# A new written-out order of turns and banks for four gated layers on one core

## The chip, the cores and the metric

The kernel runs on one core of a Trainium2 chip. The metric is the device time of one execution in microseconds (us). Three runs of the kernel before are shown; their median is the number that a change is held against.

## The reference, cut to what matters

Eight sequences (batches) of 256 rows with 128 features pass through four layers. Each layer adds a gated attention and a gated feed-forward part:

```python
x = x + tanh(g_xattn[0]) * attention0(layernorm(x), ctx)       # 16 heads of 8
x = x + tanh(g_ffn[0])   * depth0(layernorm(x))                # the best 3/4 of the rows pass a block
x = x + tanh(g_xattn[1]) * attention1(layernorm(x), ctx)
x = x + tanh(g_ffn[1])   * moe1(layernorm(x))                  # 8 experts, top 2, and a shared one
x = x + tanh(g_xattn[2]) * attention2(layernorm(x), ctx)       # causal
x = x + tanh(g_ffn[2])   * moe2(layernorm(x))                  # 8 experts of 512, top 2, and a shared one
x = x + tanh(g_xattn[3]) * attention3(layernorm(x), ctx)       # only chosen queries count
x = x + tanh(g_ffn[3])   * quantised3(layernorm(x))            # FP6 blocks
```

The change touches none of this. What matters is that every batch goes through the same long chain of small steps, and that the steps of different batches may be mixed freely.

## The kernel before, in words

**Streams.** Each batch is a stream of some 300 steps (`stream_steps`, L123 on), a list of tuples (step, layer, part): `stats` and `norm` (layer norm), `turn` (transposes), `query` and `keys` (products, then a split of each value into three bf16 parts on POOL, then transfers into `q_st` and `k_st`), `maxima` (scores for the row maxima, 8 tiles a layer), `max_parts`, `max_turn`, then eight `attend` (scores turned, exponential on ACT) and eight `weigh` (weighted sums of the values), `heads`, `heads_turn`, `project`, and the feed-forward steps. Four batches are in flight at a time, in four slots of buffers; batch b + 4 takes the slot of batch b.

**The order.** `TURNS_TAKEN` (L165) is a string of 2,410 digits. Each digit names the batch whose next step comes next. `schedule()` turns it into one list of steps, and each engine's program walks that list and issues its part of each step. So the order on TensorE, DVE, ACT, POOL and on SP's list of transfers is fixed when the kernel is built, and an engine that waits holds up all that stands behind on its own list. `BANKS_TAKEN` (L262) gives, in the same order, which of the eight PSUM banks each use takes, and from it the wait for the reader of that bank before (`bank_holders`). `SCRATCH` (L284) says in front of which steps TensorE runs how many products of zeros (`scratch`, L990 on, the product itself is L997); they write into the bank that the step is about to take, and keep the engine busy while it would wait. All three were worked out ahead of time by a planner that gives each instruction a cost; the planner is no part of the kernel.

**The routed tiles.** The third layer's feed-forward routes the rows of two batches together. When both batches of a pair (0/1, 2/3, 4/5, 6/7) have their router's choice, `place` (nine small DVE steps, L1455 to L1503) works out for each row its place among 15 tiles of 128 rows. `scatter` (L764) is eight indexed transfers from POOL that write the rows into `x_rows`. `fetch` brings them back as tiles, `turn_in` transposes them, and each tile passes `rows_hidden` (L1266, Gelu on ACT L965) and `rows_out` (L1276, copied by DVE L1751), with its expert's weights copied by POOL (`weights`, L776). `keep` writes the results into `y_rows`; `collect` (L783) is four indexed transfers a batch from POOL that gather each row's two results, and `join` adds them on DVE (L1757). POOL issues an indexed transfer itself and does nothing else meanwhile.

**Other work on the lists that the text names.** POOL also does the causal mask of the third layer's attends (the select of L790: `attend` of layer 2), the power for row norms (`key_rows` and `query_rows`, L806), the three operations of each split (L714, L717, L719), and the norm (L724, L731). In layer 3, `choose` picks the queries on DVE in 14 steps (L1623, L1625). ACT changes its function table when Gelu and the exponential alternate (ACT_TABLE_LOAD). `max_clear` and the moves into `q_st` and `k_st` stand on SP's list.

In the texts, "attend 4 of batch 7" is the step ("attend", 7, 2, 4), batch, layer and part.

Of the kernel before, what the change touches and what calls it, by code (L numbers as in the profile page):

```python
# [165 lines left out]
0003020312103121100122002000000001110103101101312132010002100010112103020202220222003100311011312031  # L166
1321231012130103113311303001320123020201021022120203200010121222110221021232111131133212221332030030
3200201312303332232032022202223310110201201100101310103303010320032210001210121120121122211301201001
3011122031222212323023211130202210303030021331013200200202020311231021210211100101211330010033321110
2030121233010232112122122122111223220302100012030022203112102110021000211100032012001001111330201110  # L170
0210211001133003001013331122100113301012123032133220121300001300000213333101131000113101101021132003
0210132130112022020103220121123113121312313133223232311313113323033131211123131111131112111311111111
1311111111111112212111311111113111211101121123323023302323203100230103012303333221123133320013303310
0003333003333313111301303003113333030033013210023033033233132133121010303131303033033300001000330023
3101100010131301101001101131130101131011111011111012033011031003033301033103331131313003010130001303
3311111333331313133301333333331300443413313433343433553335333354425442444544342224242454455325453332
4555454435532425322445242454522445423433524252424545522325353255345232322422422554423223225322442332
5232232243242452225442224443224233435343232323332343335233342225245333232523523233233325522343433222
6453364636543654645354543455435363543536445363445364434635463564466344466434666643637774574564745657
6656446656465656466565774566746565756475474556457764556747654654654775546655666767456666746564444545  # L180
5567546445547754547757576647755476776747765555775754574566655656755765755775464557467566547676664664
5665647446577767646774767746446664576576556465455564644666676546466445657666557465754746666577566675
7564676575565464775454767475657475775744775554475775646764747565466475655565747655455775555545575454
4476647476475666557555755656767567574566556657747775775777665777566555776557776655765555555555555755
5755565555555655577555577775557756555756577665777755557565765777756775677477467776767546777567474765
7477767774564667776576777775475777777777744674657757545567775755574775575757777775777777777577777477
7774444477777777757777777744547777777444777555555544455457446545544454555575464666454574555474457464
4665547544754554455767666666667774776756665646467476774767664766776766566566646765466466757766564767
6675677476576677476774775745766767775747677477656777664745475676766745646567476776674757675767774746
6657476757  # L190
# [87 lines left out]
5064751263704512673013452670123456760123745601237451603245163024516370245163702541637024516370245162  # L278
3701456237045126730451236701450423671540236014523760164502370156423742013567420135674203567423567423
5167425106725167023516723015612756230016723501670341256073412067512034120673420651734206174206145723  # L280
106451230647512306417
"""


# [1580 lines left out]
```

How the kernel before makes its waits and increments, by code:

```python
        @block.sync  # L616
# [13 lines left out]
                sp.dma_start(dst, src).then_inc(values_loaded, 16)  # L630
            for s in range(1, SLOTS):
                load_x(s, s)
                load_ctx(s, s)
            w = Walk()
            for w.i, (step, b, l, part) in enumerate(SCHEDULE):
                s = b % SLOTS
                if step == "load_x" and b + SLOTS < BATCHES:
                    sp.wait_ge(sems["xb_ready"], w.at_step("xb_ready", 1, "max_parts", b, 0, 0))
                    load_x(b + SLOTS, s)
                if step == "load_ctx" and b + SLOTS < BATCHES:
                    sp.wait_ge(sems["a_full"], w.at_step("a_full", 1, "keys", b, LAYERS - 1, 0))
                    load_ctx(b + SLOTS, s)
                if step == "load_weight3" and b == 0:
                    sp.wait_ge(sems["a_full"], w.at_step("a_full", 1, "key_mean", b, SPARSE, 0))
                    sp.dma_start(w3_sb, w3).then_inc(w3_loaded, 16)
                if step in ("keys", "query"):
                    name, terms, st, parts = (("k", K_TERMS, k_st[s], k_parts[s]) if step == "keys"
                                              else ("q", Q_TERMS, q_st[s], q_parts[s]))
                    if b < SLOTS and l == 0:
                        sp.wait_ge(*CLEARED[s])
                    if step == "keys" or b >= SPLIT_STREAMS or l > 0:
                        sp.wait_ge(sems[f"hi_ready{s}"], w.at(f"hi_ready{s}", 1))
                        move_parts(sp, terms, 0, st, parts, sems[f"{name}_moved{s}"])
```

## Time and profile before

| | before |
|---|---|
| median of 3 runs | 939.13 us (937.61 to 941.51) |
| profiled execution | 939.72 us, its span 938.0 us |
| mean granted TensorE clock | 0.961 of full speed |
| busy: TensorE, DVE, POOL, ACT | 827.9, 701.4, 596.0, 587.1 us |
| products of zeros in the written-out order | 207 (and 7 at the start) |

The span runs from the first to the last instruction; what lies around it belongs to the execution's time. Times in rows are us from the span's start, if not marked ns. A granted clock of 1.00 is 2.4 GHz, of 0.5 it is 1.2 GHz; a stretch's number is the mean over it.

### The profile page before, as it was taken

To read this page: it belongs to the slowest core of one execution; us is meant where nothing else is said; L and a number is where in the kernel's file an instruction comes from. 1 tells how busy PE (TensorE), PEld (TensorE's weight loads), DVE (VectorE), ACT (ScalarE), POOL (GpSimd) and SP (SyncE) were. 2 spreads that over 40 slices of the span, in tenths; PEclk is the share of its full clock that TensorE was granted. 3 is DMA by queue.
4 is the path that set the end of the run, shared out by engine and by line. 5 is a ranking of instruction groups with operands and counts; after the bars stand their busy time and mean duration, and the time that the engine had idled before them with its cause. 6 is when DMAs were issued, how large, how long until landed. Compare 5 with 4: busy or idle time off the path is not lost.

```text
span 938.0 us, 21784 instructions
## 1 busy us (share of the span) xinstructions
PE 827.9 (88%) x7627; PEld 525.7 (56%) x7627; DVE 701.4 (75%) x2168; ACT 587.1 (63%) x1454; POOL 596.0 (64%) x751
## 2 busy tenths in 40 slices
PE   8698899989889769997897899989999985797796
PEld 4244358845679425693344357646577954593333
DVE  7997978975752579668999998888683515746997
ACT  2586786567767436762784587776776674268180
POOL 6437548869677785667556537465878658755634
PEclk9898999999999978999999999999999998999698
DMA  5523433221121211223102121111112111311100
GB/s 137 137 77 109 122 105 91 70 64 41 46 67 33 74 35 28 70 64 82 31 21 58 42 54 39 34 36 37 28 45 66 42 49 40 88 36 41 28 4 23
DMA packets 89578, 53.90 MB, mean 57 GB/s; under 512 B 10103, under 2 KB 86416, under 8 KB 89472
## 3 DMA queue, kind: packets, MB, share of 16 engines
q1 hardware_dynamic: 82608, 40.27, 16.2%
q0 software_dynamic: 4272, 10.98, 4.1%
q10 hardware_dynamic: 2592, 1.26, 0.5%
q8 instruction: 63, 1.03, 0.5%
q14 instruction: 43, 0.35, 0.1%
HBM read 17.15 MB, written 9.04 MB: 28 GB/s over the span
## 4 chain that ended last, share of the span: by engine, by line
PE 38%; DVE 24%; POOL 16%; ACT 7%; issue 7%; DMA 5%; SPq 1%; POOLq 0%; DVEq 0%; ACTq 0%
DVE mx L1639 11%; PE banks L1059 5%; PE banks L1266 4%; PE banks L1276 4%; PE banks L1195 4%; POOL h L731 3%; ACT probs L899 3%; PE banks L1023 3%; POOL probs L783 3%; PE banks L1045 3%; PE banks L1010 3%; POOL x_rows L764 2%; PE banks L1003 2%; PE banks L1205 2%; POOL rn L806 2%
## 5 line engine op out<-in xcount | busy, mean ns | idle before, releaser
L1639 DVE TENSOR_REDUCE mx<-banks 128x4 f32<-128x1024 f32 (+1 forms) x240 | 282.9, 1214 | 17.5 <-PE banks L1023 14.1
L899 ACT ACTIVATE probs<-banks 128x512 f32<-128x512 f32 (+1 forms) x512 | 258.3, 587 | 54.8 <-PE banks L1045 53.1
L1059 PE MATMUL banks<-probs,v_aug 128*9 128x256 f32 (+1 forms) x2048 | 151.0, 374 | 16.4 <-ACT probs L899 7.2
L1023 PE MATMUL banks<-k_st,q_st 64*128 64x256 bf16 (+1 forms) x1024 | 93.3, 279 | 32.5 <-DVE mx L1639 14.5
L724 POOL TENSOR_TENSOR rstd<-veps,mhalf 128x2 f32<-128x2 f32 x64 | 46.5, 728 | 105.0 <-DVE veps L1586 104.2
L830 ACT ACTIVATE hT<-banks 128x256 f32<-128x256 f32 (+1 forms) x128 | 47.9, 383 | 102.7 <-PE banks L1003 85.1
L1045 PE MATMUL banks<-q_st,k_st 64*128 64x256 bf16 (+1 forms) x1024 | 93.9, 268 | 6.8 <-DMA q_st<-mT 3.5
L731 POOL TENSOR_SCALAR h<-xs,mv,rstd 128x128 f32<-128x128 f32 x112 | 91.7, 824 | 5.9
L806 POOL TENSOR_TENSOR rn<-ss,mhalf 128x32 f32<-128x32 f32 x16 | 88.0, 5501 | 10.3 <-DVE ss L1373 10.3
L714 POOL TENSOR_TENSOR resid<-resid,parts 128x256 f32<-128x256 f32 x64 | 42.9, 670 | 62.2 <-ACT resid L866 61.8
L1023 PEld LDWEIGHTS banks<-k_st,q_st 64*128 64x128 bf16 x1024 | 36.0, 96 | 82.1 <-DVE mx L1639 23.8
L1195 PE MATMUL banks<-hT,fc_sb 128*128 128x256 f32 x320 | 78.2, 389 | 0.0
L1045 PEld LDWEIGHTS banks<-q_st,k_st 64*128 64x128 bf16 x1024 | 33.5, 94 | 76.0 <-issue 29.5
L1059 PEld LDWEIGHTS banks<-probs,v_aug 128*9 128x9 f32 x2048 | 33.1, 89 | 73.8 <-ACT probs L899 28.4
L756 POOL TENSOR_TENSOR xs<-xs,raw 128x256 f32<-128x256 f32 x72 | 52.5, 730 | 25.8 <-ACT raw L940 23.0
L1276 PE MATMUL banks<-wall,probs 128*128 x480 | 64.2, 277 | 1.0 <-ACT probs L965 1.0
L790 POOL TENSOR_SCALAR_AFFINE_SELECT probs<-probs 128x512 f32<-128x512 f32 x64 | 40.5, 647 | 37.9 <-ACT probs L899 37.8
L1195 PEld LDWEIGHTS banks<-hT,fc_sb 128*128 128x128 f32 x320 | 58.9, 193 | 8.9 <-issue 1.1
L1751 DVE COPY raw<-banks 128x128 f32<-128x128 f32 x60 | 17.0, 288 | 61.6 <-PE banks L1276 61.5
L1276 PEld LDWEIGHTS banks<-wall,probs 128*128 128x128 f32 x480 | 58.5, 192 | 2.9 <-issue 2.7
L861 ACT ACTIVATE parts<-banks,bcol 128x256 bf16<-128x256 f32 x64 | 30.3, 474 | 43.5 <-PE banks L1073 20.9
L997 PE MATMUL banks<-zeros 128*128 128x512 bf16 x214 | 56.1, 409 | 0.0
(232 smaller groups left out, 1774.5 us busy)
## 6 DMA issues: line engine op xcount, KB each, us to landing
k_st<-parts SPq DMA_DIRECT2D x192, 64.0 KB, 2.1
q_st<-parts SPq DMA_DIRECT2D x186, 64.0 KB, 2.1
wall<-in_w POOLq DMA_DIRECT2D x16, 256.0 KB, 3.5
y_rows<-raw SPq DMA_DIRECT2D x28, 128.0 KB, 2.0
raw<-x_rows SPq DMA_DIRECT2D x12, 256.0 KB, 3.6
x_rows<-zeros SPq DMA_DIRECT2D x2, 960.0 KB, 6.6
fc_sb<-in_fc POOLq DMA_DIRECT2D x6, 256.0 KB, 4.1
x_in<-in_x SPq DMA_DIRECT2D x8, 128.0 KB, 3.8
```

Source lines behind the costliest of these rows:

```text
L731: ins = nc.gpsimd.tensor_scalar(h[s][:, r, :], (x_in if l == 0 else xs)[s][:, r, :], mv[s][:, r, 0:1], rstd[s][:, r:r + 1], ALU.subtract, ...
L756: nc.gpsimd.tensor_tensor(xs[s][:, :, :].rearrange("p t d -> p (t d)"), xs[s][:, :, :].rearrange("p t d -> p (t d)"), raw[s][:, n % OUT_RI ...
L806: nc.gpsimd.tensor_tensor(rn[s][:, :], ss[s][:, :], mhalf[:, :], ALU.pow)\
L830: nc.scalar.activation(dst, src, func).then_inc(sems["b_read"], 1)
L899: nc.scalar.activation(probs[s][:, part % UNIT_RING, 2 * a:2 * a + 2, 0:n], b_bank(w, a + 1)[:, 0:2 * n].rearrange("p (j q) -> p j q", j=2 ...
L997: nc.tensor.matmul((a_bank if kind == "a" else b_bank)(w, 1).rearrange("p (h q) -> p h q", h=2), zeros[:, 0:P], zeros_twice, start=True, s ...
L1023: ins = nc.tensor.matmul(a_bank(w, a + 1)[:, i * keys:(i + 1) * keys], head_rows(q_st, s, a, hp0 + i, r * P, P), head_rows(k_st, s, a, hp0 ...
L1045: ins = nc.tensor.matmul(b_bank(w, a + 1)[:, j * n:(j + 1) * n], head_rows(k_st, s, a, 2 * g + j, t * P, P), head_rows(q_st, s, a, 2 * g + ...
L1059: ins = nc.tensor.matmul(c_bank(b, l, u // 4)[VW * i:VW * i + VR, g % 2, q0:ROWS], v_aug[s][:, t, 4 * g + i, :], probs[s][:, u % UNIT_RING ...
L1195: ins = nc.tensor.matmul(a_bank(w, k + 1)[:, a * ROWS:(a + 1) * ROWS], fc1_sb[:, 2 * part + k, a, :], hT[s][:, :], start=True, stop=True)
L1276: ins = nc.tensor.matmul(a_bank(w, 1)[:, 0:D], rows_mid(b, part)[:, c, :], second[:, c * D:(c + 1) * D], start=c == 0, stop=c == HC - 1)
L1639: nc.vector.tensor_reduce(mx[s][:, r, :, hp0:hp0 + n], banks[:, first:first + 2, :].rearrange("p a (n k) -> p a n k", n=n), AX.X, ALU.max) ...
```

## The change

The three constants are written anew; the program around them stays as it is. Core of the diff:

```diff
 TURNS_TAKEN = """
-0003020312103121100122002000000001110103101101312132010002100010112103020202220222003100311011312031
...
+0002011123300231010103020000000001002111102113301100110012100200112210023002031031013310131012022121
...
 BANKS_TAKEN = """
-1023546016724350167234015623016745231067450201673452301672345670134570163745260123456012364503612703
...
+1023545670123457120634125634017562301474567232045132670134506715340156724536017356470134756340123451
...
 SCRATCH = {
-    ("query", 0, 0, 0): 7, ("turn", 1, 0, 0): 19, ("query", 2, 0, 0): 3, ("max_turn", 0, 0, 0): 4,
-    ("attend", 0, 1, 0): 4, ("attend", 1, 2, 0): 2, ("attend", 3, 2, 0): 10, ("maxima", 0, 3, 0): 2,
-    ("attend", 0, 3, 0): 10, ("maxima", 5, 0, 0): 18, ("turn", 2, 3, 0): 9, ("attend", 4, 0, 0): 7,
-    ("turn", 6, 0, 0): 3, ("max_turn", 4, 1, 0): 21, ("attend", 4, 1, 0): 7, ("attend", 7, 2, 0): 5,
-    ("turn", 7, 6, 0): 3, ("maxima", 4, 3, 0): 14, ("turn_in", 7, 2, 0): 11, ("turn", 6, 3, 0): 4,
-    ("max_turn", 6, 3, 0): 3, ("attend", 6, 3, 0): 2, ("attend", 7, 3, 0): 4, ("heads_turn", 7, 3, 0): 3,
-    ("turn", 5, 7, 0): 32}
+    ("query", 0, 0, 0): 7, ("max_turn", 0, 1, 0): 4, ("turn_in", 1, 2, 0): 3, ("max_turn", 3, 2, 0): 10,
+    ("turn", 0, 3, 0): 10, ("maxima", 0, 3, 0): 2, ("maxima", 5, 0, 0): 17, ("turn", 2, 3, 0): 6,
+    ("attend", 4, 0, 0): 5, ("turn", 2, 7, 0): 3, ("maxima", 6, 0, 0): 6, ("attend", 4, 1, 0): 10,
+    ("attend", 7, 2, 0): 5, ("turn", 7, 6, 0): 3, ("maxima", 5, 3, 0): 14, ("turn_in", 7, 2, 0): 14,
+    ("max_turn", 4, 3, 0): 4, ("attend", 4, 3, 0): 5, ("turn", 6, 3, 0): 5, ("turn", 7, 3, 0): 4,
+    ("attend", 6, 3, 0): 10, ("heads_turn", 7, 3, 0): 3, ("turn", 4, 7, 0): 30, ("turn", 6, 7, 0): 5}
```

The planner's cost for the issue of an indexed transfer was a quarter higher when the new strings were made. What the digits do at the places that the prediction speaks of, read off both lists:

```
DVE, batches 2/3      before  out_bias 3, place 1, max_parts 1, place 2, max_parts 1, place 3, choose 0.3, place 4 to 6, choose 0.4, place 7, 8
                      after   out_bias 3, place 1, 2, maxima 1.7, place 3, max_parts 1, place 4, max_parts 1, place 5 to 8, choose 0.0, 0.1, ...
TensorE, batch 0      before  hidden 2, max_turn 3, 10 zeros, attend 3.0, turn 0
                      after   10 zeros, max_turn 3, logits 2, hidden 2, attend 3.0, 10 zeros, turn 0
POOL, pair 4/5        before  select 6.5, scatter, select 6.6, 6.7, output 7.0, ...
                      after   scatter, select 6.5, output 7.0, select 6.6, output 7.1, ... select 6.7
TensorE, pair 4/5     before  ... rows_hidden 12, attend 7.0, 7.1, keys 6, rows_out 11, weigh 7.0 ... rows_hidden 13, ... rows_out 14
                      after   ... rows_hidden 12, rows_out 11, rows_hidden 13, rows_out 12, max_turn 7, rows_hidden 14, attend 7.0, 7.1, rows_out 13, 14, ...
POOL, after it        before  select 7.0, 7.1, keys 6, select 7.2 to 7.7, collect 5, collect 4, key_rows 7
                      after   select 7.0 to 7.3, collect 5, select 7.4 to 7.7, collect 4, keys 6, key_rows 7
ACT, near 690         before  hidden 4, ... hidden 5, logits 4, logits 5
                      after   hidden 4, logits 4, ... hidden 5, ... logits 5
TensorE, pair 6/7     between the first rows_hidden and the last rows_out
                      before  maxima 5.6, 5.7, 4.3 to 4.7, query_means 5 and 4, max_turn 5 and 4
                      after   maxima 5.7, 4.4, query_means 5, max_turn 5
TensorE, layer 3      before  heads 5, ... project 5, ... max_turn 6, heads 4, attend 6.0
                      after   ... max_turn 6, 10 zeros, attend 6.0, 6.1, heads 5, ... heads 4
```

## Rows read from the trace of the kernel before

**Rows 1.** The page's first two parts: busy time, and the granted clock by slice.

```profile
PE 827.9 (88%) x7627; PEld 525.7 (56%) x7627; DVE 701.4 (75%) x2168; ACT 587.1 (63%) x1454; POOL 596.0 (64%) x751
...
PEclk9898999999999978999999999999999998999698
```

**Rows 2.** Table by stretches: us, busy time (instructions) of PE, PEld, DVE, ACT, POOL, clock, DMA.

```profile
319.00:338.00 19.00, 14.41 (x113) 5.02 (x113) 7.20 (x34) 9.78 (x23) 12.98 (x18) 0.73 0.14 36
772.00:788.00 16.00, 7.29 (x37) 5.58 (x37) 8.01 (x41) 6.20 (x11) 14.50 (x13) 0.79 0.15 38
815.00:848.00 33.00, 32.95 (x300) 30.51 (x299) 16.42 (x34) 23.41 (x75) 16.37 (x17) 1.00 0.13 38
870.00:897.00 27.00, 21.94 (x151) 9.97 (x153) 25.05 (x41) 5.77 (x15) 14.35 (x7) 0.68 0.06 17
897.00:938.00 41.00, 32.37 (x269) 15.86 (x269) 34.46 (x159) 17.98 (x39) 18.93 (x24) 0.91 0.05 15
```

**Rows 3.** Groups by line: the indexed transfers on POOL; busy us, mean ns, idle before.

```profile
L764 POOL DMA_INDIRECT x_rows<-h,goes_to x32 | 31.7, 992 | 20.7 <-DVE tile_of L1503 11.9 <-issue 8.4 <-ACT raw L940 0.3
...
L783 POOL DMA_INDIRECT probs<-y_rows,goes_to x32 | 30.9, 967 | 19.4 <-DMA y_rows<-raw 10.8 <-issue 7.8 <-PE banks L1031 0.3
```

**Rows 4.** Timeline of PE near 320: start us, us, line, tiles, count [idle before].

```profile
319.53 2.33 PE L997 MATMUL banks<-zeros 128*128 128x512 bf16 x10
...
325.19 0.44 PE L1003 MATMUL banks<-ident,h 128*128 128x128 f32 x2 [2.78 <-POOL h L731]
...
326.94 1.04 PE L1059 MATMUL banks<-probs,v_aug 128*9 128x256 f32 x8
```

**Rows 5.** Timeline of DVE near 370: a reduction, then placing with choice steps.

```profile
367.33 1.21 DVE L1639 TENSOR_REDUCE mx<-banks 128x4 f32<-128x1024 f32 x1
...
369.20 0.17 DVE L1468 COPY raw<-banks 128x32 f32<-128x32 f32 x1
...
369.95 0.40 DVE L1625 MATCH_REPLACE8 work<-top8q,work 16x261 f32<-16x261 f32 x1
...
371.16 0.42 DVE L1623 MAX8 top8q<-work 16x8 f32<-16x261 f32 x1
...
371.99 0.17 DVE L1503 TENSOR_SCALAR tile_of<-raw 128x15 uint32<-128x15 f32 x1
```

**Rows 6.** Timeline of ACT near 757, and one piece of the chain on PE.

```profile
753.21 1.64 ACT L899 ACTIVATE probs<-banks 128x512 f32<-128x512 f32 x4
...
757.70 1.28 ACT L965 ACT_TABLE_LOAD   x1
...
761.19 1.28 ACT L899 ACT_TABLE_LOAD   x1
...
733.99 0.89 PE banks L1266 x8
```

**Rows 7.** Timeline of POOL from 763 to 784, and DVE's sums for the power.

```profile
763.63 0.63 POOL L790 TENSOR_SCALAR_AFFINE_SELECT probs<-probs 128x512 f32<-128x512 f32 x1 [4.92 <-ACT probs L899]
...
767.84 1.11 POOL L783 DMA_INDIRECT probs<-y_rows,goes_to  x1 [0.17 <-issue]
...
776.77 0.94 POOL L783 DMA_INDIRECT probs<-y_rows,goes_to  x1 [0.30 <-issue]
777.73 5.48 POOL L806 TENSOR_TENSOR rn<-ss,mhalf 128x32 f32<-128x32 f32 x1
...
773.92 0.60 DVE L1373 TENSOR_REDUCE ss<-raw 128x32 f32<-128x256 f32 x1
```

**Rows 8.** Timeline of PE at 783: the longest wait of TensorE.

```profile
783.72 1.22 PE L1093 MATMUL banks<-raw,mean_k 128*128 128x128 f32 x4 [8.19 <-DVE raw L1567]
```

**Rows 9.** Chain of waits between 819 and 832: pieces of PE among the row tiles.

```profile
820.36 0.22 PE banks L1116 x2
...
829.95 0.76 PE banks L1023 x12
```

**Rows 10.** Timeline of POOL near 850: the last pair's collect.

```profile
849.68 1.06 POOL L783 DMA_INDIRECT probs<-y_rows,goes_to  x1 [10.33 <-DMA y_rows<-raw]
```

More of the change, by code:

```diff
@@ L171 @@
[L171 to L175, printed above, removed]
@@ new lines @@
+2202001211231133312001301120012302120023123021022303002012011222112020311122111213212232233103030020
+3310320131230332032022203322223201010312012010310010110301300022100032231012112112112202113012110013
+1013221010232322010313201221123103222023003003013020210120121110230222301001111102033002121303320000
+1113120102221332212133121101231221002220012122002022013111003100110021202100021200210301101103231101
+0120201111003331013330011220010111133323021321231020023000012013001000031331012310200100000203031121
@@ new lines @@
+1221111310110321200322131321113311211223333131310113222132330313233231133211111131111221111131113211
+1131121211111111111111112113112111311111111131233333302203200032212002123013012333213312323301030023
+2303130303300333333110023113133131100333003303133303333331131303331311313333000000001000000000010110
+0102113131033111010301101111311003113011131110011310313133010003000303333101013130333130130133003313
+3131303301113313333101333310033413434113334534333353433533333544452442245422432244244544534535324255
@@ new lines @@
+4354555553443522352224445244252444234334254245222423552423435533352224552242242322244223222324523522
+4522524224322535442225434542324244523323322345333333532523323235243233235324533232332332253252435226
+5364633646534464344534545365644543353536344563444634336533454663344446643636433767664455657477664745
+4665465666564654556676674566677456555777467556655467454757454677744467654556765564654666654464667756
+4445776555465754457577745567564776454757554757655675745554566665675555764457556774675665646766456466
@@ new lines @@
+6447467565776764467777646777464466556574674556454656645464666466456664477666667566655577666655577567
+5765755476554544546445775677457764577747545457575447774667665447474566575565454674557674454745545555
+5557576675766755775575665765566556757774675576777557575776557667755575755765575567555556557555655557
+5555555555555757775655565665557667577555557567755547777557767747777477756576777677746666766476777776
+5475767547767777746577774656764777777777555576457674477774755764744557575575775777777777777777777777
@@ L191 @@
+7777775777777777747777777777577745744445754554545455565755445544644446664464444545756547465755454454
+5547445444477556766665664665477766665664677776656766564676676577757667667646766566656654677776466477
+5746767467757755777676774766777577574677646754776747465745676767456465764676747674674467766757577675
+6764547577
 """
@@ new lines @@
+1725564701234567120374502317045172301457623456012234576012360451762307456023764507123640512365401725
+3601475316045713620457362073451672034675120345601724372567012345670145230167452367014523645701236745
+6701234253674201523460145237601764501723614576123457610234571023570235670231756023176021375601234650
+1452301634561203470562103457612035467210356721036572013650147325014673520143675201436705214367025143
+6702514367025413670521436701523674501236745401236754012367541236750146237400156347204516723451060123
```

50 lines of the change are left out of this document (13 added, 37 removed).

## The prediction

> **What bounds the kernel now.** I read the page first. TensorE is busy for 88% of the span and DVE for 75%, and the granted clock is at 9 or 10 tenths in most slices, with one 6 and one 7 among them [rows 1]. So no engine bounds the whole: what counts is in which stretch an engine stands still and whether that stretch can give anything back. The second view is therefore the table by stretches. The reader is to see two kinds there. From 815 to 848 TensorE is busy for 32.95 of 33.00 us: whatever leaves that stretch shortens it. From 870 to 897 the bound is DVE (25.05 of 27 us), and around 319 and 772 TensorE idles or runs at the lower of its two clock levels [rows 2].
>
> The third view is the groups by line, for what the change is planned around: one indexed transfer keeps POOL busy for 0.99 us (scatter, L764) or 0.97 us (collect, L783), and behind most of them stands an issue gap, 8.4 us over 28 and 7.8 us over 27 [rows 3], so about 0.3 us each. The slot that the order has to leave free is thus near 1.27 us. Eight of them take 9.9 us on POOL from the first start at 767.84 to the last end at 777.72 [rows 7], 1.23 us each.
>
> The change keeps every product, transfer and vector operation. It moves them on five queues, in small steps (the largest by 115 places of 2,410), gives 1,544 of 1,821 uses of a PSUM bank another bank, and runs 185 products of zeros for 207. So the sum is made place by place; where the order differs but TensorE is full before and after, I count nothing, since the same work stands in the same stretch.
>
> **The places.**
>
> *319 to 338, batch 0 enters its last layer.* Before, ten products of zeros run at 319.53, then TensorE waits 2.78 us for batch 0's normed rows [rows 4], and the granted clock of this stretch is 0.73 [rows 2]: (1 - 0.73) x 19 = 5.1 us of full-speed work lost, or some 10 us at 1.2 GHz. The new order has ten products of zeros a little earlier, in front of max_turn of batch 3, and ten in front of the turn that waited, so the wait is filled by 10 x 0.233 = 2.3 us of products [rows 4]. No row shows the clock with that filling. The ends are nothing (the clock falls all the same) and -5.1. What limits the gain is that the chain is TensorE's only in part: batch 0's second row tile still needs POOL and ACT. I take -1.5, nearer to nothing, since the 1.04 us for 8 products at 326.94 [rows 4] is followed by waits of other engines; both ends stay for the range. The Trainium skill's page "TensorE: Matmul & The Clock Gate" (section "HAM oscillation") counts a stretch at half clock as half of it lost; by it this place gives the whole 5.1 and the sum below would be 929.6. The trace has the 0.73, but not a chain that is TensorE's throughout.
>
> *369 to 373, the rows of batches 2 and 3 are placed.* DVE runs the small place operations from 369.20 to 372.16 with two steps of the choice of queries between them, 0.40 and 0.42 us, and POOL's scatter waits for the last [rows 5]. In the new order the choice starts behind the placing: -0.8, and about -0.1 for a paused step that stood ahead. But a reduction of maxima of 1.21 us [rows 5], which stood ahead of an output's bias, now stands between the second and third place operation; it is neutral if the bias, and what follows it, comes that much earlier, else +1.2. I take -0.9. Ends: +0.4 and -1.2. What is late next: the choice itself, 14 steps, needed only by the heads of batch 0.
>
> *704 to 784, pair 4/5.* Three things. First, TensorE did the last three tiles of this pair between the attends of batch 7; ACT changed its function table for that at 757.70 and 761.19, 1.28 us each [rows 6]. Now the four steps of 0.89 us [rows 6] that lie ahead of attend 0 of batch 7 finish the tiles, so the exponentials start about 3.6 us later (756.8 for 753.21), but all follow each other: two attends in 1.64 us [rows 6], four in 3.3, to 760.1, and select 3 ends at 760.8. Second, POOL's collect of batch 5 now stands ahead of select 4 of batch 7: four issues, 4.9 us, to 765.7; select 4 starts then, for 763.63 before [rows 7], 2.1 us late, and the products of attend 4 behind it on TensorE stand for that time. Selects 4 to 7 follow in 2.6 us (0.64 each), to 768.3. Third, collect 4 (4.9) and the three splits of keys 6 (1.9) end at 775.1, and the 5.5 us power for batch 7's key rows starts there; before it started at 777.73, since both collects stood ahead of it, though its sums were ready at 774.52 [rows 7]. So -2.6 at this point; I take -2.4, as the sums themselves may come at 775. What waited was TensorE, 8.19 us at 783.72 [rows 8]. Ends: -4 (the rows of the pair come earlier too, since the scatter now goes ahead of one select of batch 6) and +5 (the collect stands without its keep, see the rivals). The two table changes come back near 690, where the exponential of batch 4's router moves between two hidden layers: 2 x 1.28 on ACT, beside a TensorE whose own order there is ahead by about as much; 0, up to +1.3.
>
> *815 to 848, pair 6/7.* TensorE is full, so each step moved out counts: five score steps of batches 4 and 5 (three such take 0.76 us), one turn of query means (0.22) [rows 9] and one turn of maxima, taken as the same 0.22. 5 x 0.25 + 0.44 = -1.7. Who waits: the attends of batch 4, behind three later reductions on DVE. Their cover is the collect's 10 us on POOL, which waits 10.33 us for this very stretch [rows 10]; without the cover, three reductions of 1.21 us [rows 5] would cost some 3.6 us. Ends: 0 and -2.5.
>
> *The rest.* The opening loses 26 products of zeros ahead of the first attends; TensorE waits there for loads and DVE, so 0, with ends of -1 and +3. From 870 on, heads of batches 5 and 4 move behind max_turn of batch 6, and ten products of zeros stand in front of its first attend. The work is the same, moved from a stretch at 0.68 into one at 0.91 [rows 2]; DVE bounds the first. 0, with ends of -4 and +4. SP: its list of transfers hardly changes order; the keep of pair 4/5 and the one of 6/7 are issued a few places earlier, ahead of clears that nobody waits for soon. 0.
>
> **The sum.** -1.5 - 0.9 - 2.4 - 1.7 = -6.5. The profiled execution took 939.72 us, 1.72 beyond its span and 0.59 above the median of 939.13. 939.72 - 6.5 = 933.2; I give **933.0 us**.
>
> **The rivals.**
>
> *It is absorbed (0.32).* Each gain is an earlier arrival, and the next stretch has a limit of its own: after 319 it is reductions on DVE, after 772 it is a chain of placing and a scatter. Then only the place where TensorE is full pays, 1.7 us: 937.5 with rounding, within the 0.5% (4.7 us) that a measurement can tell from no change. For: the chain passes through all engines. Against: the 8.19 us wait on TensorE has POOL alone behind it [rows 8].
>
> *POOL's list stands (0.12), the slower side.* At two places selects now queue behind indexed issues: select 5 of batch 6 behind eight (9.9 us), select 4 of batch 7 behind four (4.9). I counted 2.1 us of these 14.8 as uncovered. If TensorE runs out of other work at both, 12.7 us more: 945.7. It decides from 10.8 us uncovered on. For: POOL once waited 10.33 us for a keep with its list behind it [rows 10]. Against: at the first place the new order gives TensorE outputs and hidden layers to do meanwhile.
>
> *The clock stays low to the end (0.08).* From 870 to 897 it is 0.68, from 897 on 0.91 [rows 2]: 7.4 us of the last 41 are at half. If the other 33.6 are too, 16.8 x 32.37/41 = 13.3 us are lost: 946.3. For: 22 products fewer in all, and the Trainium skill's same page (section "What's actually happening") says that the throttled state is the default and activity releases it. Against: this stretch gets more products of zeros, not fewer.
>
> **How the numbers follow.** The forecast has 0.48. Its own range is 926 (the far ends of 319, 704 and 870, not all at once) to 937. With the absorbed case and most of the POOL case the range goes to 945. Left out are the clock case and what lies under 926. Faster by over 0.5% is under 934.4: 0.48. Same: 0.32. Slower: 0.12 + 0.08 = 0.20.
>
> **What would show it.** Right: no wait of TensorE over 5 us near 784, but one of 2 to 5 us before the fifth group of weighted sums of batch 7; no table changes between the exponentials of batch 7; a clock over 0.8 in the 19 us around batch 0's last turn into layer 3; the last row stretch some 1.7 us shorter. Wrong: waits of TensorE on selects of 6 us and more; a clock under 0.9 over the opening's second half; or gains at these places and an end that is not earlier, which would make it the absorbed case.

## The result, and the profile after

| | before | after |
|---|---|---|
| median (runs) | 938.37 us (937.2 to 941.51, 4 runs) | 951.87 us (950.28 to 958.29, 4 runs) |
| ratio | 1 | 1.0151, 95% interval 1.0098 to 1.0205 |
| profiled execution, its span | 939.72, 938.0 us | 952.19, 950.5 us |
| mean granted TensorE clock | 0.961 | 0.945 |

The changed kernel is 13.5 us slower where 6 us less were forecast. Line numbers after are one lower than before. The page's first two parts (busy time, and the granted clock in 40 slices) answer to [rows 1]:

```profile
PE 834.1 (88%) x7605; PEld 529.0 (56%) x7605; DVE 703.0 (74%) x2168; ACT 586.7 (62%) x1454; POOL 598.1 (63%) x751
...
PEclk8799999999999979998898999999999978899899
```

TensorE is busy for 6.2 us more with 22 products fewer. That is the clock: at 0.961 some 2 x 0.039 x 938 = 73 us of the span were at 1.2 GHz, at 0.945 it is 105 us. Two executions of the kernel after had a mean clock of 0.952 and took 950.28 and 951.54 us; 13 executions of the kernel before with the same clock, in the experiments, took 941.49 to 947.6 us, with a median of 943.8. So about half of the difference stays at an equal clock: it is not the clock alone.

The table by stretches, which answers to [rows 2] (us, busy time and instructions of PE, PEld, DVE, ACT, POOL, then clock, DMA share, GB/s). The stretches are moved by the delay that had come about by then; the one at 764 holds batch 7's attends, which stood ahead of the row at 772 before:

```profile
319.00:338.00 19.00, 14.98 (x136) 7.06 (x135) 11.18 (x45) 11.88 (x28) 13.96 (x20) 1.00 0.15 39
338.00:441.00 103.00, 89.30 (x757) 62.03 (x757) 79.72 (x257) 54.12 (x140) 71.35 (x79) 0.88 0.21 58
...
764.00:782.00 18.00, 11.25 (x92) 6.29 (x88) 3.18 (x10) 6.68 (x17) 12.71 (x17) 0.62 0.16 42
...
826.00:860.00 34.00, 33.05 (x305) 30.26 (x303) 12.65 (x26) 24.39 (x76) 13.35 (x15) 1.00 0.11 31
...
882.00:909.00 27.00, 20.90 (x186) 9.45 (x180) 25.57 (x45) 7.88 (x18) 14.30 (x7) 0.87 0.07 18
909.00:950.00 41.00, 30.57 (x270) 15.39 (x266) 35.02 (x158) 17.48 (x38) 18.93 (x24) 0.98 0.05 15
```

The reader sees the filled wait at work: from 319 to 338 the clock is 1.00, where it was 0.73. But in the next 103 us it is 0.88; the same stretch of the kernel before, 102 us long, had 0.95. The stretch of batch 7's attends got worse: TensorE is busy for 11.25 of 18 us, at a clock of 0.62. The same attends before:

```profile
757.00:774.00 17.00, 14.24 (x140) 10.17 (x140) 3.99 (x16) 12.01 (x27) 9.11 (x12) 1.00 0.21 56
```

The attends of the kernel after on TensorE (timeline of PE: start us, us, line, tiles, count, and in brackets the idle time before and its releaser):

```profile
765.43 0.62 PE L1058 MATMUL banks<-probs,v_aug 128*9 128x256 f32 x8 [1.32 <-POOL probs L789]
...
771.73 1.04 PE L1058 MATMUL banks<-probs,v_aug 128*9 128x256 f32 x8 [4.02 <-POOL probs L789]
...
775.19 1.47 PE L1058 MATMUL banks<-probs,v_aug 128*9 128x256 f32 x16 [1.00 <-POOL probs L789]
...
790.98 1.06 PE L1092 MATMUL banks<-raw,mean_k 128*128 128x128 f32 x4 [3.60 <-DVE raw L1566]
```

and on POOL:

```profile
751.99 5.47 POOL L805 TENSOR_TENSOR rn<-ss,mhalf 128x32 f32<-128x32 f32 x1 [1.01 <-DVE ss L1372]
...
766.13 1.11 POOL L782 DMA_INDIRECT probs<-y_rows,goes_to  x1 [0.17 <-issue]
...
771.01 1.25 POOL L789 TENSOR_SCALAR_AFFINE_SELECT probs<-probs 128x512 f32<-128x512 f32 x2
774.50 1.22 POOL L789 TENSOR_SCALAR_AFFINE_SELECT probs<-probs 128x512 f32<-128x512 f32 x2 [2.24 <-ACT probs L898]
...
785.00 5.46 POOL L805 TENSOR_TENSOR rn<-ss,mhalf 128x32 f32<-128x32 f32 x1 [2.53 <-DVE ss L1372]
```

The wait of 8.19 us [rows 8] has shrunk to 3.60, as forecast. But the power for batch 7's key rows starts at 785.00, where it started at 777.73 [rows 7], and now it waits for DVE's sums: the attends themselves came late, with waits of TensorE (1.32, 4.02 and 1.00 us) that the tiles had filled before. One power, that of batch 6's key rows (751.99), stands right ahead of the attends; before it started at 736.3, beside the tiles.

How late the changed kernel is, step by step, shows where the rest came about. I took the time of each step in both traces and, near each time of the trace before, the median of the differences on TensorE (the lag): 1.8 us at 18 us, 2.0 at 190, 3.9 at 211, 0.8 at 258, 1.3 at 445, 4.2 at 457, 6.0 at 556, 2.8 at 675, 3.8 at 704, 11.4 at 812, 11.7 at the end. So there are several losses, two stretches that gain, and one big step behind 740. A lag of 1 to 3 us can be one profile's clock, as the runs below show.

### The profile page after: what moved, and what is told of

It reads as the page before. It is cut to its first block, busy times and chain, and to the rows that moved or that the text cites. A ratio compares the mean times of both kernels' runs of the same rounds, so it can differ in the third digit from the quotient of the medians.

```text
span 950.5 us, 21743 instructions
## 1 busy us (share of the span) xinstructions
PE 834.1 (88%) x7605; PEld 529.0 (56%) x7605; DVE 703.0 (74%) x2168; ACT 586.7 (62%) x1454; POOL 598.1 (63%) x751
## 4 chain that ended last, share of the span: by engine, by line
PE 43%; DVE 21%; POOL 13%; ACT 7%; issue 7%; DMA 5%; SPq 3%; POOLq 0%; ACTq 0%; DVEq 0%
DVE mx L1638 10%; PE banks L1058 7%; PE banks L1044 4%; PE banks L1265 4%; PE banks L1022 4%; PE banks L1275 3%; PE banks L1009 3%; DMA q_st<-parts 3%; PE banks L1194 3%; ACT probs L898 3%; POOL h L730 3%; SPq L604 3%; PE banks L1165 2%; PE banks L996 2%; PE banks L1002 2%
## 5 line engine op out<-in xcount | busy, mean ns | idle before, releaser
L1044 PE MATMUL banks<-q_st,k_st 64*128 64x256 bf16 (+1 forms) x1024 | 96.5, 272 | 10.7 <-DMA q_st<-mT 4.6
```

The costliest lines, as they stand in the source:

```text
L1044: ins = nc.tensor.matmul(b_bank(w, a + 1)[:, j * n:(j + 1) * n], head_rows(k_st, s, a, 2 * g + j, t * P, P), head_rows(q_st, s, a, 2 * g + ...
```

## The experiments

Both orders hold the same steps. At 0, 569, 626, 1,435, 1,740, 1,831 and 2,063 steps the two have taken exactly the same set, so that pieces of one can be set into the other, each with its banks and its products of zeros. Behind a cut, 0 to 14 uses of banks take another bank than written, where the neighbour still held it. The runs fall into four groups; those of a group share a chip and the runs of the kernel before, whose medians are 941.61, 940.95, 942.24 and 941.9 us (19, 30, 33 and 29 runs), so ratios are compared.

**One piece back, one piece alone.** The piece is steps 1,831 to 2,062, the stretch of pair 4/5.

```diff
 # e1_old_pair45, against the kernel after (one line of the piece)
-5557576675766755775575665765566556757774675576777557575776557667755575755765575567555556557555655557
+5557576675766755775575665765566567574566556657747775775777665777566555776557776655765555555555555755
```

> The changed kernel, with the steps 1,831 to 2,062 of its order (about 704 to 810 us: the tiles of pair 4/5, batch 7's attends, both collects, the placing of pair 6/7) put back as they stood before, its zeros with them. Theory A, the order in this stretch costs most: between the two cuts TensorE fell behind by a further 7.6 us (3.8 at the first, 11.4 at the second), so about 944 us. Theory B, the 22 missing products of zeros let the clock fall in many places: at most 2 us come back, 949 to 952. Theory C, a delay there is given back by slack later: 950 or more.

```diff
 # e2_new_pair45, against the kernel before (one line of the piece)
-4476647476475666557555755656767567574566556657747775775777665777566555776557776655765555555555555755
+4476647476475666557555755656767556757774675576777557575776557667755575755765575567555556557555655557
```

> The kernel before, with only the steps 1,831 to 2,062 in the new order, its zeros with them. A: 938.4 + 7.6, about 946 us. B: 938 to 940, for the zeros of this stretch number 25 in the old and 22 in the new order. C: 938 to 940.

Measured: the piece back 953.02 us, ratio 1.0113 (1.0067 to 1.0158), for 1.0151 with the new piece; the piece alone 945.68 us, 1.0045 (1.0019 to 1.0072). So the piece costs about 0.4%, half of what A said, and most of the loss is elsewhere: A falls as the main cause. C, that slack gives the delay back, fits the first run and not the second. The traces say why the lag had overstated it: two landmarks inside the piece, the first indexed transfer of pair 4/5's scatter and the key mean of batch 7, show the part that is the order's. Timeline of POOL and of PE, first of the kernel after, then of the piece alone:

```profile
707.11 1.11 POOL L763 DMA_INDIRECT x_rows<-h,goes_to  x1 [0.90 <-DVE tile_of L1502]
```

```profile
703.65 1.11 POOL L764 DMA_INDIRECT x_rows<-h,goes_to  x1 [1.02 <-DVE tile_of L1503]
...
768.26 1.04 PE L1059 MATMUL banks<-probs,v_aug 128*9 128x256 f32 x8 [4.15 <-POOL probs L790]
...
781.15 5.46 POOL L806 TENSOR_TENSOR rn<-ss,mhalf 128x32 f32<-128x32 f32 x1 [2.14 <-DVE ss L1373]
...
787.13 1.22 PE L1093 MATMUL banks<-raw,mean_k 128*128 128x128 f32 x4 [3.60 <-DVE raw L1567]
```

From landmark to landmark it is 790.98 - 707.11 = 83.9 us and 787.13 - 703.65 = 83.5 in the new order; in the old one 783.72 - 704.28 = 79.4 before, and 80.2 with the piece set back. Seven more profiles with the old order and its zeros here have 79.4 to 79.9, and one has 81.5. The order costs about 4 us here in both directions. The lag behind 785 us is another thing: the run with the piece set back lost 3.6 us more there, too (13.6 at 812 for 10.0 at 795).

**The zeros of before in the new order.**

```diff
 # e3_old_zeros, against the kernel after
 SCRATCH = {
-    ("query", 0, 0, 0): 7, ("max_turn", 0, 1, 0): 4, ("turn_in", 1, 2, 0): 3, ("max_turn", 3, 2, 0): 10,
...
+    ("query", 0, 0, 0): 7, ("turn", 1, 0, 0): 19, ("query", 2, 0, 0): 3, ("max_turn", 0, 0, 0): 4,
...
```

> The changed kernel with the 207 products of zeros of before, each in front of the same step as before, and none of the 185 new ones. A: 949 to 953 us, the opening 2 us better, the stretch at 326 worse. B: 938 to 945, and the share of the time at the lower clock falls from 107 us back to about 75.

Measured: 981.14 us, ratio 1.0387 (1.0325 to 1.0449), mean clock of the profile 0.934. Neither theory expected it. More zeros gave a lower clock, so B, the count of zeros, falls. In front of a step that has another place in the order, they no longer fill a wait but hold up what stands behind. The 21 in front of batch 4's turn of maxima show it; PE before, then DVE and PE in this run:

```profile
514.09 4.71 PE L997 MATMUL banks<-zeros 128*128 128x512 bf16 x21
520.04 0.28 PE L1147 MATMUL banks<-mask_b,m_parts 128*32 128x128 bf16 x2 [1.24 <-DVE m_parts L1652]
```

```profile
535.18 0.18 DVE L1652 SCALAR_TENSOR_TENSOR m_parts<-mx,m_parts 128x32 bf16<-128x32 f32 x1
...
537.78 7.01 PE L997 MATMUL banks<-zeros 128*128 128x512 bf16 x21
544.72 0.29 PE L1147 MATMUL banks<-mask_b,m_parts 128*32 128x128 bf16 x2
```

Before, the turn still waits for DVE's maxima when the zeros are done; here the maxima are ready 2.4 us before the zeros start, and the turn stands behind all 7.01 us of them.

**The two stretches that gained.**

```diff
 # e4_mix, against the kernel before (first lines of its two pieces)
-0210211001133003001013331122100113301012123032133220121300001300000213333101131000113101101021132003
+0210211001133003001013331122100113301012123032133220121300001300000210031331012310200100000203031121
...
-6656446656465656466565774566746565756475474556457764556747654654654775546655666767456666746564444545
+6656446656465656466565774566746565755777467556655467454757454677744467654556765564654666654464667756
```

> The kernel before, with the two stretches in which the changed kernel gained on it: steps 569 to 625 (240 to 258 us, lag 3.4 to 0.7) and 1,435 to 1,739 (555 to 675 us, lag 6.0 to 2.8), their zeros with them. If gains in a stretch last: 938.4 - 2.7 - 3.2 = 932.5 us. If they are only delays from elsewhere that had slack to be made good: 938 to 940.

Measured: 945.14 us, ratio 1.0031 (0.9997 to 1.0065). The second piece brought its gain in the trace (lag 4.7 at 556, 1.9 at 675); the first one, alone behind the old order, lost 4 us at 258 where it had gained 2.4 in the kernel after. So a gain seems to belong to the order that stands ahead of it, too.

**First part, middle part, and the same kernel again.**

```diff
 # e5_new_first, against the kernel before (first line; steps 0 to 568 are new)
-0003020312103121100122002000000001110103101101312132010002100010112103020202220222003100311011312031
+0002011123300231010103020000000001002111102113301100110012100200112210023002031031013310131012022121
```

> The kernel before, with only its first 569 steps (to about 241 us) in the new order, 28 products of zeros fewer. Theory A2, losses add up stretch by stretch: the lag at the cut was 3.2 and 4.9 us in two profiles of this prefix, so 3 to 5 us more than before. Theory D, only the lower clock makes the difference and it comes from anywhere: no clear difference at an equal mean clock.

```diff
 # e6_new_middle, against the kernel before (first line; steps 569 to 1,830 are new)
-0210211001133003001013331122100113301012123032133220121300001300000213333101131000113101101021132003
+0210211001133003001013331122100113301012123032133220121300001300000210031331012310200100000203031121
```

> The kernel before, with only the steps 569 to 1,830 (241 to 704 us) in the new order, 15 products of zeros fewer. A2: +0.6 to +2.8 us by the lags at the two cuts (3.2 to 3.8, and 4.9 to 7.7). D: the same as before at an equal clock.

> The kernel before once more, unchanged, as a measure of how far two profiles and two sets of runs of one program differ. Expected by all: ratio 1 within 0.3%; its lag against the first profile shows how much of 2 to 5 us in a stretch is the clock's chance.

(The last one has no edit.) Measured: first part 943.62 us, 1.0038 (1.0015 to 1.0060); middle part 945.96 us, 1.0056 (1.0035 to 1.0077); the kernel again 940.89 us, 1.0003 (0.9978 to 1.0028). The losses of the first part, the middle and the piece behind 704 are of one size, 3.6, 5.3 and 4.2 us, and their sum is that of the whole, as A2 said, though A2 had the middle at 0.6 to 2.8. Part of them is the clock's: the mean clocks are 0.952, 0.951 and, for the kernel before in the same group, 0.956. Held against a straight line of time over clock through the 30 executions of the kernel before, I estimate 1.4 us for the first part and 3.3 for the middle at an equal clock; so D, the clock alone, falls for the middle at least. The kernel again also shows the noise of a profile: its span is 935.0 us for 938.0, and against its own first profile its lag went to -3.4 us at 342 and back to 0.0 at 795.

For the middle, the table by stretches, before and after, from the attends of batches 4 and 5 to those of batch 5's second layer, seems to show one cause:

```profile
456.00:557.00 101.00, 89.04 (x909) 43.12 (x905) 97.46 (x290) 68.26 (x147) 54.44 (x67) 1.00 0.16 41
```

```profile
460.00:563.00 103.00, 90.68 (x904) 44.60 (x900) 97.62 (x289) 67.93 (x147) 53.72 (x67) 0.95 0.16 40
```

DVE does the same 97.5 us of work and is the fullest engine; it idles for 3.5 us before and for 5.4 after. But the clock differs as well, and other profiles with the old order in this stretch look like the kernel after. This is the run with the tiles ahead (below), whose order is that of before up to 740 us:

```profile
453.80:557.30 103.50, 92.49 (x909) 45.58 (x905) 97.45 (x290) 68.42 (x147) 54.41 (x67) 0.95 0.16 40
```

Of the 13 profiles with the old order and its zeros here, seven at a clock of 0.95 to 0.97 took 103.0 to 104.7 us for the same work, and six at 0.98 to 1.00 took 100.9 to 101.4. So these 2 us come and go with the clock and need no moved step. Where the middle loses the rest stays open; in its own profile the lag rose from -0.2 us at 241 to 5.4 at 262, and later changes largely cancel.

**What the piece behind 704 consists of.** Three runs on top of the piece alone, or in its place.

```diff
 # e8_collect_late, against e2_new_pair45: collect 5 behind attend 7 of batch 7
-5555555555555757775655565665557667577555557567755547777557767747777477756576777677746666766476777776
+5555555555555757775655565665557667577555557567755547777577677477775477756576777677746666766476777776
```

> The kernel before with the steps 1,831 to 2,062 in the new order, as in the run that cost 4 us, but the collect of batch 5 is moved behind the eight selects of batch 7, next to the collect of batch 4. Theory A3, POOL's indexed issues ahead of selects make TensorE stand: the 4.0 us wait at 771.7 goes, and 3 to 4 us come back, about 942 on a chip where the kernel before takes 941.6. Theory A4, the tiles drawn ahead of the attends make the loss and the collect is only where it shows: 0 to 1 us come back, 945.

```diff
 # e11_collect_joins_late, against e2_new_pair45: its two joins behind key_rows of batch 7 as well
-5555555555555757775655565665557667577555557567755547777557767747777477756576777677746666766476777776
+5555555555555757775655565665557667577555557567755547777577677477775477767677767775546666766476777776
```

> The kernel before with the steps 1,831 to 2,062 in the new order (4 us slower), but the collect of batch 5 behind the eight selects of batch 7 and its two joins behind the sums for batch 7's key rows, so that neither POOL nor DVE stands for it. If the early collect with its joins is the loss: 3 to 4 us come back, no difference from before. If the tiles ahead are: 4 us slower than before, as with the collect alone moved.

```diff
 # e10_tiles_ahead, against the kernel before: the last tiles ahead of the attends, nothing else
-5755565555555655577555577775557756555756577665777755557565765777756775677477467776767546777567474765
+5755565555555655577555577775557756555756555555776655557777767677776775677477467776767546777567474765
```

> The kernel before, in which only the last pieces of the tiles of pair 4/5 are drawn ahead: rows_out 11 to 14, rows_hidden 13 and 14 and their keeps stand in front of or between the first two attends of batch 7 and no more between the later ones. The collect, the joins and the power of batch 6's key rows stand as before. Theory A4: 3 to 4 us slower. The prediction's sum (the attends start 3.6 us later, without table changes; the power behind them waits for POOL anyway): between 2 us faster and no change. Theory A5, it is the power of batch 6's key rows, later on POOL and ahead of max_parts, that delays the attends: no change.

Measured: collect late 945.87 us, 1.0051 (1.0030 to 1.0071); collect and joins late 945.41 us, 1.0034 (1.0009 to 1.0060); tiles ahead alone 942.12 us, 1.0013 (0.9991 to 1.0036). The first two bring nothing that can be told from the piece itself (1.0045), so the 4 us wait behind the four issues is not what the piece costs: with the collect late, DVE stood at the join and TensorE waited 3.42 us for the heads behind it, and from landmark to landmark the two runs have 85.9 and 86.1 us, more than the piece's 83.5. Timeline of PE with the collect late:

```profile
778.58 0.69 PE L1003 MATMUL banks<-ident,resid 128*128 128x128 f32 x2 [3.42 <-DVE resid L1667]
```

The tiles alone cost 1.2 us, at most 3.4: A4, as the whole explanation, falls too. Timeline of POOL and PE with the tiles ahead:

```profile
704.47 1.11 POOL L764 DMA_INDIRECT x_rows<-h,goes_to  x1 [0.17 <-issue]
...
758.33 1.23 POOL L790 TENSOR_SCALAR_AFFINE_SELECT probs<-probs 128x512 f32<-128x512 f32 x2 [5.73 <-ACT probs L899]
...
768.31 1.22 POOL L790 TENSOR_SCALAR_AFFINE_SELECT probs<-probs 128x512 f32<-128x512 f32 x2 [1.14 <-ACT probs L899]
...
779.61 5.48 POOL L806 TENSOR_TENSOR rn<-ss,mhalf 128x32 f32<-128x32 f32 x1
...
785.60 1.22 PE L1093 MATMUL banks<-raw,mean_k 128*128 128x128 f32 x4 [6.55 <-DVE raw L1567]
```

Measured from the scatter, the first select starts 3.8 us later than before (754.37 - 704.28), about as the prediction had it; the last two follow closely, the collects end at 779.6, and from landmark to landmark it is 81.1 us, 1.7 more than before.

The rest was to be the keys of batch 6. In the old order their product, split and mean are done among the tiles at 752; in the new one they stand between the weighted sums and the heads of batch 7.

```diff
 # e13_tiles_ahead_keys_late, against e10_tiles_ahead
-5755565555555655577555577775557756555756555555776655557777767677776775677477467776767546777567474765
+5755565555555655577555577775557756555756555555775555677777777777757747467677767766666546777567474765
```

> The kernel before, with the last tiles of pair 4/5 ahead (which alone measured +0.1%) and batch 6's keys moved as in the new order: their product stands between the last weighted sums of batch 7 and its heads on TensorE, their split behind the collects and ahead of the power on POOL. Theory A6, the keys are the rest of the loss (about 2 us of products at the lower clock on TensorE, 1.75 us of splits on POOL): 3 to 4.5 us slower than before. Otherwise: 0 to 1.5 us slower, as with the tiles alone.

Measured: 945.1 us, 1.0033 (1.0011 to 1.0055), 3.1 us, at the lower end of A6; the interval, 1.0 to 5.2 us, reaches into the other case (0 to 1.5) too, so A6 is likely and not shown. Timeline of POOL, then PE:

```profile
705.89 1.11 POOL L764 DMA_INDIRECT x_rows<-h,goes_to  x1 [0.17 <-issue]
...
780.04 0.68 POOL L714 TENSOR_TENSOR resid<-resid,parts 128x256 f32<-128x256 f32 x1
780.79 0.48 POOL L717 CAST parts<-resid 128x256 bf16<-128x256 f32 x1
781.35 0.67 POOL L719 TENSOR_TENSOR parts<-resid,parts 128x256 bf16<-128x256 f32 x1
...
781.98 5.46 POOL L806 TENSOR_TENSOR rn<-ss,mhalf 128x32 f32<-128x32 f32 x1
...
788.19 1.20 PE L1093 MATMUL banks<-raw,mean_k 128*128 128x128 f32 x4 [2.10 <-DVE raw L1567]
```

The three operations of the split stand between the last collect and the power, and push it back by 2.0 us; from landmark to landmark it is 82.3 us. So of the 4.1 us, by one profile each, 1.7 are the tiles', 1.2 the keys', and 1.2 stay unassigned.

**The new end alone, no zeros at all, and the two gains.**

```diff
 # e15_new_end, against the kernel before (first line that differs; steps from 2,063 on are new)
-7477767774564667776576777775475777777777744674657757545567775755574775575757777775777777777577777477
+7477767774564667776576777775475777777777744674657757545567775754744557575575775777777777777777777777
```

> The kernel before with only the steps from 2,063 on (from about 812 us) in the new order, 21 products of zeros more. By the sum of parts (1.51% less 0.38, 0.56 and 0.45): +0.1%, 1 us. By the prediction's sum for the last row stretch: -1.7 us. By the lags (the old end gains 2.4 us on the first profile near 890 us in every other profile, the new end none): +2 us.

Measured: 946.29 us, 1.0041 (1.0017 to 1.0065). The end costs 3.9 us, where the profile after seemed to show nothing (lag 11.4 and 11.7). It was hidden by the one profile of before: from the scatter of pair 6/7 (799.71) to the end of its span it has 138.3 us, but the 12 other profiles with the old end and its zeros have 135.9 to 138.2, half of them under 136.8; with the new end it is 141.3 to 143.4 (three profiles). What is late in it is batch 7's row maxima. Timeline of POOL and DVE, of the kernel before again and of the new end alone:

```profile
799.13 1.10 POOL L764 DMA_INDIRECT x_rows<-h,goes_to  x1 [0.98 <-DVE tile_of L1503]
...
893.01 1.19 DVE L1639 TENSOR_REDUCE mx<-banks 128x4 f32<-128x1024 f32 x1
...
894.55 0.16 DVE L1649 TENSOR_SCALAR m_parts<-mx 128x32 bf16<-128x32 f32 x1
```

```profile
802.09 1.10 POOL L764 DMA_INDIRECT x_rows<-h,goes_to  x1 [0.98 <-DVE tile_of L1503]
...
898.33 3.47 DVE L1639 TENSOR_REDUCE mx<-banks 128x4 f32<-128x1024 f32 x3
...
902.47 0.15 DVE L1649 TENSOR_SCALAR m_parts<-mx 128x32 bf16<-128x32 f32 x1
```

The split of the maxima starts 95.4 us behind the scatter in the one and 100.4 in the other. Of these 5.0 us, 2.4 are there when DVE comes to batch 6's first reduction (869.73 and 875.09); the rest comes about while five steps of batch 6's choice stand ahead of the split, where there were two, on the engine that is the fullest here. Batch 7 is the batch that ends last. No run moved these choices alone.

The end also holds the row tiles of pair 6/7. From their first product to their last it is 28.7 us in all four profiles with the new end and 31.05 to 31.11 in the 13 with the old one and its zeros: that stretch did become 2.4 us shorter. But its first tile comes later. Issue of its rows' transfer and TensorE, before and after:

```profile
811.56 2.01 SPq L672 DMA_DIRECT2D raw<-x_rows  x4
...
814.36 0.66 PE L1260 MATMUL banks<-ident,raw 128*128 128x128 f32 x4 [1.76 <-DMA raw<-x_rows]
```

```profile
819.25 2.01 SPq L671 DMA_DIRECT2D raw<-x_rows  x4
819.41 1.04 PE L1022 MATMUL banks<-k_st,q_st 64*128 64x256 bf16 x8 [2.21 <-DVE mx L1638]
820.38 5.62 PE L996 MATMUL banks<-zeros 128*128 128x512 bf16 x14
825.84 0.60 PE L1259 MATMUL banks<-ident,raw 128*128 128x128 f32 x4
```

The tiles' turn starts 2.8 us behind the issue before, as soon as the rows have come, and 6.6 us after, behind 14 products of zeros. From the scatter to the first tile's product it is 15.6 us before and 19.0 after (18.3 with the new end alone, at most 16.8 in the other 12 profiles with the old one).

```diff
 # e16_no_zeros, against the kernel before
 SCRATCH = {
-    ("query", 0, 0, 0): 7, ("turn", 1, 0, 0): 19, ("query", 2, 0, 0): 3, ("max_turn", 0, 0, 0): 4,
...
+}
```

> The kernel before without any of its 207 products of zeros in the order (the 7 at the very start stay). If they keep the clock up and fill waits: slower, by up to 15 us, and the mean clock falls below 0.94. If they mostly hold up the work behind them, as the 26 in the opening: 2 to 6 us faster.

Measured: 956.91 us, 1.0151 (1.0117 to 1.0186), mean clock of the profile 0.906. The page's granted clock by slice:

```profile
PEclk8699999999999878995998899999999987699795
```

Some 2 x 0.094 x 956 = 180 us are at the lower level, for 73 in the first profile of before: in their own order the zeros are worth 14 us. The change only leaves work out, so what makes it slower is most likely the lower clock; no run has it at an equal clock.

```diff
 # e12_no_opening_zeros, against the kernel before
 SCRATCH = {
-    ("query", 0, 0, 0): 7, ("turn", 1, 0, 0): 19, ("query", 2, 0, 0): 3, ("max_turn", 0, 0, 0): 4,
-    ("attend", 0, 1, 0): 4, ("attend", 1, 2, 0): 2, ("attend", 3, 2, 0): 10, ("maxima", 0, 3, 0): 2,
+    ("query", 0, 0, 0): 7, ("attend", 0, 1, 0): 4, ("attend", 1, 2, 0): 2, ("attend", 3, 2, 0): 10,
+    ("maxima", 0, 3, 0): 2, ("attend", 0, 3, 0): 10, ("maxima", 5, 0, 0): 18, ("turn", 2, 3, 0): 9,
...
```

> The kernel before without the 26 products of zeros that the new order lacks in the opening (19 ahead of batch 1's first turn, 3 ahead of batch 2's query, 4 ahead of batch 0's max_turn), nothing else. The prediction's sum: 0, -1 to +3. By the lag behind the opening in two profiles of the new prefix (0.8 to 1.8 us, with the lower clock from 14.6 to 21.4 us as well): +1 to +2 us.

```diff
 # e9_gain_alone, against the kernel before (first line; steps 1,435 to 1,739 are new)
-6656446656465656466565774566746565756475474556457764556747654654654775546655666767456666746564444545
+6656446656465656466565774566746565755777467556655467454757454677744467654556765564654666654464667756
```

> The kernel before, with only the steps 1,435 to 1,739 (555 to 675 us) in the new order. In four profiles of this stretch in the new order the lag fell by 2.4 to 3.4 us, in the old order it moved by -0.1 to +1.0. If that is the order: 2.5 to 3 us faster than before, about 938 on a chip where before takes 941, a version that beats both. If the gain belongs to what stands ahead of it (later arrival, same end): within 1 us of before.

> The kernel before with the steps 1,435 to 1,739 in the new order (0.9961 alone) and without 26 products of zeros in the opening (0.9960 alone). If the two are independent: 0.992, about 934.5 where before takes 942. If both only hit the same chance of the clock: 0.996.

(The last has both edits.) Measured: without the 26 opening zeros 937.65 us, 0.9960 (0.9940 to 0.9980); with steps 1,435 to 1,739 new 938.8 us, 0.9961 (0.9939 to 0.9982); with both 936.71 us, 0.9958 (0.9938 to 0.9977). Each beats the kernel before by 0.4%, and so the one after by more; together they bring no more than one. And the stretch that alone gains 0.4% is part of the middle, which as a whole loses 0.56%: costs of pieces do not simply add. The stretch from 555 to 675, before and in the run with it alone:

```profile
555.50:675.00 119.50, 114.21 (x1134) 73.44 (x1129) 97.07 (x281) 90.76 (x231) 74.19 (x103) 1.00 0.12 31
```

```profile
560.50:677.30 116.80, 112.94 (x1134) 73.58 (x1129) 97.75 (x281) 89.71 (x230) 74.66 (x103) 1.00 0.12 32
```

It is 2.7 us shorter, with TensorE idle for 3.9 us in place of 5.3 and busy for 1.3 us less. For the opening zeros the one profile (941.38 us, above that kernel's median) doesn't show where the gain lies; that stays open, and with it why the two don't add.

## Why the prediction was wrong

*The rest, counted as 0.* This is the step that failed. The prediction costed four places and said that where TensorE is full before and after, it counts nothing, "since the same work stands in the same stretch". The first 569 steps cost 3.6 us, the middle 5.3 and the end 3.9, 0.38, 0.56 and 0.41%, against the forecast of 0 for all but 319, 369 and 815. With the piece behind 704 (0.45%) the sum is 1.80%, and the whole measured 1.51% (0.98 to 2.05). The reason given did not hold for much of the order: from 456 to 557 and at 870 [rows 2] DVE is fuller than TensorE, as it is from 20 to 45 us (23.0 of 25 us, TensorE 16.5). Which moved step costs how much there is not shown. The opening's missing zeros, given -1 to +3, measured -3.8 us alone, so what else moved in the first part cost more than its 3.6, if the two add.

*704 to 784, -2.4 us.* Measured +4.1 by the landmarks, +4.2 by the time of the piece alone. The first select did start some 4 us later and the wait of 8.19 us did shrink. The sum had DVE's sums for the power ready by 775; in the kernel after, whose scatter starts 2.8 us later, the power waits for them until 785.00, some 7 us later than that. Wrong was that the exponentials "all follow each other": TensorE's list has the weighted sums of one pair of attends ahead of the products of the next, so a late select holds up the next attends as well. And the sum had "three splits of keys 6" ahead of the power, but not their product ahead of the heads on TensorE, nor that the tiles had been the work that filled the round trips: without them TensorE waited for selects and its clock was 0.62. The runs give 1.7 of the 4.1 us to the tiles and 1.2 to the keys.

*319 to 338, -1.5 us.* Right inside the stretch: the clock was 1.00 for 0.73, and the lag fell from 2.6 at 311 us to -0.5 at 342. Then the clock of the next 103 us was 0.88 for 0.95, and the lag was back at 1.4 by 428: -1.2 in all, most of the gain given back. The two other profiles with the new order and zeros here, the piece set back and the middle, gave as good as all of it back (lags of 4.8, 2.1, 4.7 and 4.9, 2.9, 5.1 at the same three times). The old order's own lag moves by 1 us here from profile to profile. By the rule that the prediction weighed (the Trainium skill, "TensorE: Matmul & The Clock Gate", section "HAM oscillation") this place was worth the whole -5.1. The trace, with -3.1 inside the stretch and -1.2 behind it, does not agree. No run had this place alone.

*369 to 373 and 815 to 848.* The first, -0.9, is smaller than what two profiles of one kernel differ by, and wasn't tried alone. The second was to save 1.7 us, and the stretch itself saved 2.4. But from the scatter of pair 6/7 to the product of its last tile it is 46.7 us before and 47.8 after: one of the score steps that left now stands ahead of the first tile and waits for DVE, and the zeros behind it hold the tile up. That these steps would cost nothing where they went is what was wrong; the end as a whole costs 3.9 us.

*The rivals.* "POOL's list stands" named the place of the 4.02 us wait, but the run with the collect behind the selects shows that this wait is not the loss. "The clock stays low to the end" is wrong: 0.98 from 909 on. The absorbed case gave no loss at all. The slower side had 0.20; none of its cases was many small losses at once, which is what happened.

*The signs.* All five signs given for being right were there: a wait of 3.60 us at batch 7's key mean, one of 4.02 before its fifth group of weighted sums, no table change between its exponentials (ACT loads its table at 759.46 and next at 784.00), a clock of 1.00 from 319 to 338, and the row tiles 2.4 us shorter. They test the places that were costed and say nothing of the rest. Of the signs for being wrong, a low clock in the opening was there: 0.66 from 20 to 45 us for 0.86 before.

## What to carry to other kernels

When an order is written anew, treat each stretch as a chance of a loss, not as 0: here three quarters of the pieces' cost stand outside the stretch from 704 to 812. Give a sign that covers the whole, too, for all signs at the costed places came true in a kernel that is slower. Pieces of two orders can be exchanged wherever both have taken the same set of steps; that prices each stretch in a few runs, and here found a mix that beats both. Filler in front of a step belongs to that step's place: move the step, and place the filler anew. Profile the old version more than once before reading differences of 2 to 3 us out of a pair of traces: one profile's luck hid the cost of the end, and made 2 us of the clock look like DVE's wait from 456 to 557.

## What the runs showed of the hardware

One program on one chip took 934.66 to 946.24 us in 19 executions, and the time goes with the granted clock: 0.972 in the fastest, 0.953 in the slowest. In two profiles of this program about as much time was at 1.2 GHz (clock 0.961 in both), but from 870 to 897 the one was at 0.68, where the other was at 0.79, and it was 3 us longer there than the other. Zeros in front of a TensorE wait are worth 14 us in the order they were planned for, and 26 of them cost 4; the same 207 in the new order took its ratio from 1.0151 to 1.0387. So they belong to one order, and their count alone does not tell what they do.
